# Weight loads on POOL's queue, weighted values right after the scores, and scatters that wait for them

## What is computed

```python
h = _layer_norm(x, ln1_w, ln1_b)
q, k, v = (einsum('btc,hcs->bhts', h, W) for W in (Wq, Wk, Wv))      # 4 heads of 32
wei = softmax(where(causal, einsum('bhts,bhus->bhtu', q, k) * scale, NEG_INF))
attn = einsum('bhtu,bhus->bhts', wei, v).transpose(0, 2, 1, 3).reshape(B, T, C)
x = x + attn @ Wo + bo
nx = _layer_norm(x, ln2_w, ln2_b)
noisy = nx @ Wr + br + noise * softplus(nx @ Wn + bn)
router_out = softmax(where(top 2 of 8 experts, noisy, NEG_INF))
for e in range(8):
    fe = relu(nx @ W1[e] + b1[e]) @ W2[e] + b2[e]                    # 128 -> 512 -> 128
    expert_out += router_out[..., e:e + 1] * fe
final = where(sigmoid(nx @ Wsk + bsk) <= 0.5, x + expert_out, x)
```

## Time and profile before

| | us |
|---|---|
| median of three runs | 997.89 |
| their lowest and highest | 996.54, 998.24 |
| the profiled execution | 997.75 |
| its span, first to last instruction | 995.2 |

### The profile page before, as it was taken

The page is one execution under the profiler, slowest core; times in us unless marked ns, Lnnn a source line. Parts: engine busy times, 40 slices in busy tenths (PEclk is TensorE's granted clock), DMA queues, the critical chain, the costliest instruction groups (busy, mean ns, idle before and its releaser), DMA issues.

```text
span 995.2 us, 19253 instructions
## 1 busy us (share of the span) xinstructions
PE 651.0 (65%) x4844; PEld 473.0 (48%) x4844; DVE 556.9 (56%) x2095; ACT 504.6 (51%) x1081; POOL 425.6 (43%) x490
## 2 busy tenths in 40 slices
PE   2477766775776766775775785419999999971000
PEld 1245553553553544553553553317777777760000
DVE  3364553553553553554554554337777777751998
ACT  3465554554554563554555543318778787760000
POOL 5223354354345354345345344633556565543000
PEclk9688777778678687678678776559999999996555
DMA  8744233233233242233233234466767667632998
GB/s 225 234 146 129 75 92 88 73 88 90 70 90 89 69 115 67 73 83 94 67 84 100 56 93 118 95 216 234 237 214 239 223 224 236 214 113 90 320 336 283
DMA packets 143292, 143.85 MB, mean 145 GB/s; under 512 B 25250, under 2 KB 113411, under 8 KB 143264
## 3 DMA queue, kind: packets, MB, share of 16 engines
q1 hardware_dynamic: 107744, 107.84, 36.6%
q10 hardware_dynamic: 23232, 19.93, 6.2%
q0 software_dynamic: 12288, 15.77, 5.1%
HBM read 73.86 MB, written 62.78 MB: 137 GB/s over the span
## 4 chain that ended last, share of the span: by engine, by line
PE 33%; issue 14%; DVE 6%; SPq 3%; another core or an unknown queue 2%; ACT 2%; DVEq 2%; DMA 1%; POOL 0%; POOLq 0%; ACTq 0%
PE ps L573 5%; PE ps L612 3%; PE ps L702 3%; PE ps L700 3%; DVE z L1160 2%; PE ps L701 2%; PE ps L712 2%; PE ps L713 2%; PE ps L714 2%; PE ps L621 2%; PE ps L655 2%; DVE z L1165 2%; PE ps L604 2%; PE ps L602 1%
## 5 line engine op out<-in xcount | busy, mean ns | idle before, releaser
L1238 POOL DMA_INDIRECT expert_rows<-pay,rows_of x256 | 252.4, 986 | 321.4 <-DVE rows_of L1050 248.8
L1255 POOL DMA_INDIRECT expert_results<-z,words x128 | 130.9, 1022 | 121.9 <-DVE z L1127 89.6
L743 ACT ACTIVATE z<-xres,shift,rstd 128x128 f32 (+1 forms) x256 | 105.0, 482 | 48.0 <-DVE shift L989 37.5
L612 PE MATMUL ps<-hlo,v_sb 128*32 128x128 f32 x1024 | 79.9, 383 | 72.1 <-issue 68.3
L995 DVE TENSOR_REDUCE smax<-ps 128x16 f32<-128x512 f32 x32 | 22.1, 691 | 182.1 <-remote 182.1
L1141 DVE TENSOR_TENSOR hlo<-h,hhi 128x512 fp32r<-128x512 f32 x128 | 88.6, 692 | 59.6 <-ACT hhi L887 48.5
L885 ACT ACTIVATE h<-ps,w1x 128x512 f32<-128x512 f32 x128 | 88.8, 694 | 47.9 <-PE ps L702 37.5
L612 PEld LDWEIGHTS ps<-hlo,v_sb 128*32 128x32 f32 x1024 | 49.8, 152 | 123.7 <-issue 116.4
L887 ACT ACTIVATE hhi<-ps,w1x 128x512 fp32r<-128x512 f32 x128 | 88.4, 691 | 0.0
L787 ACT ACTIVATE qT<-ps 128x512 f32<-128x512 f32 x32 | 19.0, 593 | 125.5 <-remote 110.9
L602 PE MATMUL ps<-hT,wq 128*128 128x512 f32 x64 | 46.1, 766 | 45.0 <-issue 38.4
(11 more groups left out here) (156 smaller groups left out, 1408.1 us busy)
## 6 DMA issues: line engine op xcount, KB each, us to landing
w1x<-split_weights SPq DMA_DIRECT2D x33, 514.0 KB
w2x<-split_weights SPq DMA_DIRECT2D x33, 512.5 KB
expert_results<-zeros SPq DMA_DIRECT2D x32, 512.0 KB
pay<-expert_rows SPq DMA_DIRECT2D x33, 264.0 KB
xres<-in_r_x SPq DMA_DIRECT2D x32, 256.0 KB, 5.1
hhi<-kT SPq DMA_DIRECT2D x128, 64.0 KB
hlo<-pT SPq DMA_DIRECT2D x128, 64.0 KB
hhi<-expert_results SPq DMA_DIRECT2D x16, 512.0 KB, 6.0
```

The source lines that it names most:

```text
L612: m = nc.tensor.matmul(ps[h * HS:(h + 1) * HS, O_BANK, j * P:(j + 1) * P], v_sb[:, odd, j, h * HS:(h + 1) * HS], p_bd[:, :, (j * H + h) * ...
L743: m = nc.scalar.activation(z[:, j:j + 1], tile(xres, n, j), ACT.Identity, bias=shift[:, which, j:j + 1], scale=rstd[:, which, j:j + 1])
L1238: g.indirect_dma_start(rows, bass.IndirectOffsetOnAxis(ap=rows_of[:, odd, k * J + j:k * J + j + 1], axis=0), pay[:, odd, k, j, :], None, b ...
L1255: g.indirect_dma_start(results, bass.IndirectOffsetOnAxis(ap=words[:, slot, j:j + 1], axis=0), yrow[slot][:, j, :], None, bounds_check=K * ...
```

## The change

- **PE's order.** The 32 matmuls of the weighted values stand right behind the scores, ahead of q and k.
- **POOL's hold.** Before a group's eight scatters (group n = t - 3, step t) POOL also waits for `s_o_made` of n + 4, which is the weighted values of group t, done in PE's step t + 1.
- **The rank** is summed by 6 matmuls in place of 15, with the running counts in one more column block, so that DVE copies `fill` (instead of adding).
- **The payload** of group n is copied in step n + 3 (before: n + 2).
- **Waits of DVE** for z1 and z2 move from ahead of the statistics to ahead of `rstd`.
- **First steps.** `load_raw` goes to POOL's queue: four experts ahead of the loop, the others as their slot is free. `store_cut` goes to SP's queue, behind `spread_k`. DVE zeroes `k_bd` (t = -2) and `p_bd` (t = -1). The scale of the first norm has a semaphore of its own, so it waits for two small loads and not for the q, k and v weights.

```diff
--- before.py
+++ after.py
@@ -205,6 +205,7 @@
...
         s_p_bd = sem("p_bd")
+        s_norm1_in = sem("norm1_in")
@@ -344,7 +345,7 @@
...
         SENT = 16 * K * J
-        QKV = 16 * 5
+        QKV = 16 * 3
@@ -458,6 +459,8 @@
...
                     spread_k(n)
+                for e in splits(t - 1):
+                    store_cut(e)
@@ -467,21 +470,19 @@
...
 
-            def load_raw(e):
-                slot = e % 4
-                sp.dma_start(raws[slot][:, 0:HF], W1[e]).then_inc(raw_in[slot], 16)
-                sp.dma_start(raws[slot][:, HF:2 * HF].rearrange("p (k c) -> p k c", c=C),
-                             W2[e].rearrange("(k p) c -> p k c", p=P)).then_inc(raw_in[slot], 16)
+            def store_cut(e):
+                sp.wait_ge(s_cut_low, e + 1)
+                for w, split in enumerate((wsplit1, wsplit2)):
+                    sp.dma_start(split[e * P:(e + 1) * P, 0:2 * HF], wcut[e % 4][:, w].bitcast(F32)
+                                 ).then_inc(cut_out[e % 4], 16)
...
             load_first(0, s_x_early[0])
-            sp.dma_start(norm1[:, 0:1], ln1_w.unsqueeze(1)).then_inc(s_qkv_in, 16)
-            sp.dma_start(norm1[:, 1:2], ln1_b.unsqueeze(1)).then_inc(s_qkv_in, 16)
+            sp.dma_start(norm1[:, 0:1], ln1_w.unsqueeze(1)).then_inc(s_norm1_in, 16)
+            sp.dma_start(norm1[:, 1:2], ln1_b.unsqueeze(1)).then_inc(s_norm1_in, 16)
...
             load_first(1, s_x_early[1])
-            load_raw(0)
-            load_raw(1)
@@ -594,15 +595,6 @@
...
                     m.then_inc(s_s_made, 1)
-                n = t + 1
-                if live(n):
-                    pe.wait_ge(s_hT_made, n + 1)
-                    if isinstance(n, int) and n == 0:
-                        pe.wait_ge(s_qkv_in, QKV)
-                    nc.tensor.matmul(ps[:, 4, :], wq[:].rearrange("c h s -> c (h s)"), hT[:],
-                                     start=True, stop=True).then_inc(s_q_made, 1)
-                    nc.tensor.matmul(ps[:, 6, :], wk[:].rearrange("c h s -> c (h s)"), hT[:],
-                                     start=True, stop=True).then_inc(s_k_made, 1)
@@ -616,6 +608,15 @@
...
                 if live(n):
+                    pe.wait_ge(s_hT_made, n + 1)
+                    if isinstance(n, int) and n == 0:
+                        pe.wait_ge(s_qkv_in, QKV)
+                    nc.tensor.matmul(ps[:, 4, :], wq[:].rearrange("c h s -> c (h s)"), hT[:],
+                                     start=True, stop=True).then_inc(s_q_made, 1)
+                    nc.tensor.matmul(ps[:, 6, :], wk[:].rearrange("c h s -> c (h s)"), hT[:],
+                                     start=True, stop=True).then_inc(s_k_made, 1)
+                n = t + 1
+                if live(n):
@@ -625,17 +626,14 @@
...
                     wait(pe, s_route, n * ROUTE)
-                    nc.tensor.matmul(ps[:, 7, 384:384 + J * E1].rearrange("p (j e) -> p j e", e=E1), ones_row[:],
-                                     fill[0:1].unsqueeze(1).to_broadcast([1, J, E1]), start=True, stop=False)
-                    for j in range(J):
-                        rank = ps[:, 7, 384 + j * E1:384 + (j + 1) * E1]
-                        nc.tensor.matmul(rank, before[:], hot_any[:, j, :], start=False, stop=False)
-                        for i in range(j):
-                            nc.tensor.matmul(rank, ones[:], hot_any[:, i, :], start=False,
-                                             stop=(i == j - 1 and j == J - 1))
-                    for j in range(J):
-                        m = nc.tensor.matmul(ps[:, 7, 384 + J * E1:384 + (J + 1) * E1], ones[:], hot_any[:, j, :],
-                                             start=(j == 0), stop=(j == J - 1))
+                    counts = ps[:, 7, 384:384 + (J + 1) * E1].rearrange("p (j e) -> p j e", e=E1)
+                    nc.tensor.matmul(counts, ones_row[:], fill[0:1].unsqueeze(1).to_broadcast([1, J + 1, E1]),
+                                     start=True, stop=False)
+                    nc.tensor.matmul(counts[:, 0:J], before[:], hot_any[:], start=False, stop=False)
+                    for i in range(J):
+                        m = nc.tensor.matmul(counts[:, i + 1:J + 1], ones[:],
+                                             hot_any[:, i].unsqueeze(1).to_broadcast([P, J - i, E1]),
+                                             start=False, stop=(i == J - 1))
@@ -819,12 +817,12 @@
...
                                          ACT.Copy).then_inc(s_v_copied, 1)
-                n = t - 2
-                if live(n):
-                    wait(act, sent[par], pair(n, par, SENT))
+                n = t - 3
+                if live(n):
+                    wait(act, sent[odd], pair(n, odd, SENT))
...
                         act.wait_ge(s_pay_zeroed, 1)
-                    nc.scalar.activation(pay[:, par, :, :, 0:C], z2[:, par].unsqueeze(1).to_broadcast([P, K, J, C]),
+                    nc.scalar.activation(pay[:, odd, :, :, 0:C], z2[:, odd].unsqueeze(1).to_broadcast([P, K, J, C]),
@@ -836,10 +834,6 @@
...
                     nc.scalar.activation(tiles(top2, n), top[:, :, 0:K], ACT.Copy).then_inc(s_top_kept, 1)
-                for e in splits(t - 1):
-                    store_cut(e)
-                    if e + 4 < E:
-                        load_raw(e + 4)
@@ -847,20 +841,6 @@
...
 
-            def load_raw(e):
-                slot = e % 4
-                act.dma_start(raws[slot][:, 0:HF], W1[e]).then_inc(raw_in[slot], 16)
-                act.dma_start(raws[slot][:, HF:2 * HF].rearrange("p (k c) -> p k c", c=C),
-                              W2[e].rearrange("(k p) c -> p k c", p=P)).then_inc(raw_in[slot], 16)
-
-            def store_cut(e):
-                act.wait_ge(s_cut_low, e + 1)
-                for w, split in enumerate((wsplit1, wsplit2)):
-                    act.dma_start(split[e * P:(e + 1) * P, 0:2 * HF], wcut[e % 4][:, w].bitcast(F32)
-                                  ).then_inc(cut_out[e % 4], 16)
-
-            load_raw(2)
-            load_raw(3)
@@ -946,11 +926,9 @@
...
                             apart(dve, (x_in[par], pair(t + 2, par, 16) + 16 - 8 * EARLY))
-                        wait(dve, s_z1, t + 2)
...
                             apart(dve, (s_x1_made, n + 1))
-                            wait(dve, s_z2, n)
@@ -960,8 +938,11 @@
...
                 if isinstance(t, int) and t == -2:
-                    turn_scale(norm1, s_qkv_in, QKV)
+                    ev.memset(k_bd, 0.0).then_inc(s_bd_zeroed, 1)
+                    turn_scale(norm1, s_norm1_in, 32)
                     make_masks()
+                if isinstance(t, int) and t == -1:
+                    ev.memset(p_bd, 0.0).then_inc(s_bd_zeroed, 1)
@@ -983,6 +964,10 @@
...
                     dve.wait_ge(s_norm, base + 3)
+                    if live(t + 2):
+                        wait(dve, s_z1, t + 2)
+                    if live(t - 2):
+                        wait(dve, s_z2, t - 2)
@@ -1032,8 +1017,7 @@
...
                     dve.wait_ge(s_rank_made, n + 1)
-                    ev.tensor_tensor(fill[:], fill[:], ps[:, 7, 384 + J * E1:384 + (J + 1) * E1],
-                                     ALU.add).then_inc(s_route, 1)
+                    ev.tensor_copy(fill[:], ps[:, 7, 384 + J * E1:384 + (J + 1) * E1]).then_inc(s_route, 1)
@@ -1177,6 +1161,13 @@
...
             g = nc.gpsimd
+
+            def load_raw(e):
+                slot = e % 4
+                g.dma_start(raws[slot][:, 0:HF], W1[e]).then_inc(raw_in[slot], 16)
+                g.dma_start(raws[slot][:, HF:2 * HF].rearrange("p (k c) -> p k c", c=C),
+                            W2[e].rearrange("(k p) c -> p k c", p=P)).then_inc(raw_in[slot], 16)
+
@@ -1215,8 +1206,8 @@
...
                    allow_small_or_imprecise_dtypes=True).then_inc(s_token_next, 1)
-            g.memset(k_bd, 0.0).then_inc(s_bd_zeroed, 1)
-            g.memset(p_bd, 0.0).then_inc(s_bd_zeroed, 1)
+            for e in range(4):
+                load_raw(e)
@@ -1232,7 +1223,8 @@
...
                     apart(pool, (s_route, n * ROUTE + ROUTE),
-                                (s_pay_made, n + 1))
+                                (s_pay_made, n + 1),
+                                (s_o_made, upto(n + 4)))
@@ -1242,6 +1234,9 @@
...
                 slot = e % 4
+                if 1 <= e <= 4:
+                    pool.wait_ge(s_cut_low, e)
+                    load_raw(e + 3)
```

## The result

The kernel before took 998.69 us (median of 6 runs) beside the changed kernel's **953.13 us** (944.21 to 956.34): a ratio of 0.954, 95% interval 0.949 to 0.958. The direction is the predicted one; the time lies 8 us above the range of 852 to 945. The profiled execution took 956.34 us, span 954.6.

The account below looks back on a forecast made before the run. The prediction took 32-column matmuls, stalled while POOL scatters, to bound the pipeline at 18.7 us a group. Its sum was 997.75 - 99.5 (period) - 4 (first steps) - 4 (drain) = 890 us, range 852 to 945.

Parts of the forecast that it names:

- Mechanism: In the pipeline, POOL's scatters hold back matmuls on 32 columns some ten microseconds; full-width ones pass with a small lag.
- Period: Time per group in the pipeline: 18.7 us falls to 15.0 (13.5 to 16.5), worth -99.5 us over 27 distances.
- The loop through the hold: Weighted values' end, 0.8 us to first scatter, 10.0 of scatters, 1.98 to release, then scores and weighted values: 15.0 us.
- 1.98 + 1.5 + 0.7: After a group's last scatter: narrow matmuls finish (1.98 us), weighted values run (1.5), ACT and DVE hand-offs lag (0.7).
- First steps: Start of the pipeline: moved loads, stores and zeroing free ACT and start scores earlier, -4 us, between -12 and +8.
- the sign of the +8: First four steps: spreads of pT landing behind the stores in SP's queue would show the +8 us bound.
- Drain: From the pipeline's last mask to its last scatter's end: 64.6 us becomes 60.3, -4 us, from -8 to +2.
- Counted as worth nothing: In the pipeline, the later payload copy, the shorter rank and DVE's moved waits were each put at nothing.
- central case: Only narrow matmuls stall, so the hold shortens the pipeline's groups to 15.0 us: 890 us, recorded bounds 850 to 935, chance 0.74.
- Rival 1: Inside the pipeline's scatter stretch every signal lags, not PE's alone: 17.5 us a group, 957 us; chance 0.14.
- Rival 2: Scatters stall all of PE's pipeline work, decided once over 5.9 us must wait: 22.3 us a group, 1095 us; chance 0.08.
- Rival 3: No contention in the pipeline, the hold only moves the stall: groups stay at 18.7 us, 990 to 998 us; chance 0.04.

Follow-up runs that it names:

- e12: The changed kernel without POOL's hold, with a test stretch of matmul and ScalarE trials ahead of its pipeline: 1260.9 us, one execution (kernel before 997.1).
- e4: The kernel before with the first steps' part of the change alone: 774.4 us against 782.5, ratio 0.990.
- e7: The kernel before with first steps and POOL's hold, old order, payload not moved, plus an added test stretch: 1157.6 us, one execution (kernel before 782.4).
- e11: The kernel before with first steps, POOL's hold and the later payload, in the old order of TensorE: 784.7 us against 782.0, ratio 1.004.
- e9: The changed kernel without POOL's hold, with a test stretch ahead of its pipeline: 926.3 us, one execution (kernel before 784.2).
- e5: The changed kernel itself, run again beside the kernel before in another sitting: 794.3 us against 781.8, ratio 1.016.

## Why the prediction was wrong, point by point

- **Mechanism.** It took the kind of matmul for the cause. The step that failed is "so full-width matmuls pass, with a small lag; those on 32 columns don't". The earlier trace rows showed stretches with few instructions beside the scatters (15 matmuls of the rank; 4.6 matmuls a microsecond in the experts' stage, 903 in 195 us), and I read their width instead of their number. The runs showed in its place that full-width matmuls are held back as well: z2's transposes by 4.5 us and the projection by 6.5 us in the changed kernel's step, and 8.7 us over e12's trial of short full-width matmuls.
- **Period, 15.0 predicted, 17.0 measured: 54 of the 66 us by which the profiled execution lies over 890.** The loop through the hold is right, with 0.9 us from weighted values to scatter and 10.0 us of scatters. The term mis-sized is the stretch from the last scatter's end to the next weighted values' end: 1.98 + 1.5 + 0.7 = 4.2 us by the sum, 6.0 measured on average (17.0 - 10.1 - 0.9). In the sum the scores were released at once; in the step above the late z2 transposes and projection first let the logits (402.16) and the next transposes go, and only then the mask (404.43). Work that was put beside the scatters did not fit beside them.
- **What the sum got right.** smax's wait vanished, POOL is released by the weighted values, q and k finish inside the scatters, the first mask comes at 27.0 us (before 31.3). DVE wasn't next.
- **First steps: -4 predicted, +1.2 measured**, inside the bounds of -12 to +8, by the very wait named as the sign of the +8. Under the old order the same edits bring 8.1 us (e4, a free sitting): the two halves of the change spoil each other.
- **Drain: -4 predicted, +4.2 measured.** The bound of +2 was too tight. Of the sum's 60.3 us, the 16.7 to the first of the last four groups' scatters became 20.2 (550.6 to 570.8), and the four groups took 48.7 in place of 43.6, with gaps between them. The hold alone costs 6.3 us of drain in a free sitting.
- **Counted as worth nothing:** the rank and the moved waits were never run alone, so this isn't shown for them. For the payload it was wrong: its move breaks a ring worth 9 us a group (e7 and e11, free sittings).
- **The range.** The central case's own bounds (periods of 13.5 to 16.5 us, first steps -12 to +8, drain -8 to +2) add up to 838 to 949 us, not to the recorded 850 to 935. The measured time lies above this too.
- **Rivals.** Rival 1, "inside the stretch every signal lags, not PE's alone", gave 957 us and had 0.14; it comes nearest in mechanism, since ACT is held back too (e12). That its time is so near is in part luck: its 17.5 us a group is too long by 13 us over 27 distances, and its -8 for first steps and drain too low by 13. Rival 2's point of decision never came, since some of PE's work does pass. Rival 3, no contention, was given 0.04; it is what seven of eleven sittings show, with its consequence, a change that gains nothing (+1.6%).
- Of the Trainium skill's rule ("SBUF — State Buffer", "Who interferes with whom"), that no DMA contends with a compute engine and that TensorE and ScalarE wait on nobody: the free sittings agree (in e9 the 32-column batches take 18.6 us beside scatters and 18.4 beside plain DMAs), the blocked ones don't (10.9 and 5.7 us for a burst of 8), though no run tells whether it is the memory's ports that are in the way.

**What stays open** is what makes a sitting blocked. It is constant within one, changes on the same chip, concerns both engines tried (PE, ACT), and needs POOL's scatters. The loading of instructions is an unlikely cause: the DMA view of the changed kernel from 91 to 550 us has 9 packets on the instruction queues, too few for 27 groups that all wait. Every time here comes with a record of its execution, so no run tells whether the recording itself takes part. The Trainium skill describes such a path ("NOTIFIC — the notification-queue block", section "7.1 Overflow: three behaviours, one of which stalls the engine"): the records that engines leave go through a block whose inner stages push back when they fill and can throttle an engine. That would fit a count of instructions of any kind; no run here shows it.

## What to carry to other kernels

A stall that follows one engine's instructions may be counted in the other engines' instructions and not in their kind or time: before a schedule is built on "this kind passes", compare the number of instructions that each observed stretch held. A wait added to an engine that releases buffers can close a ring through a third engine's queue; follow each semaphore of the held transfers to whoever waits for it, and move those waits with it. And run the kernel before beside every measurement, on more than one occasion: the same change was worth -4.6% in one kind of sitting and +1.6% in the other.

## What the runs showed of the hardware that was not expected

- The same kernel on the same chip took 999 us in one sitting and 782 in another. In the changed kernel (953 and 794 us) the scatters of the pipeline account for nearly all of such a difference (812.7 and 804.3 us without them).
- In a blocked sitting eight scatters (0.97 us each, 1.28 apart) hold back both engines tried (e12): after some 28 to 65 of TensorE's instructions its signals come late, and ScalarE advances by four instructions in 1.42 us. Eight plain DMAs issued by POOL in 4.33 us hold back nobody.
- TensorE's records don't show it: of the projection's matmuls the record ends 6.5 us before DVE read their result, with "remote" as the only trace of it.
- The granted clock in the pipeline follows the gaps: 0.76 before, 0.81 after, 0.95 in e5's free sitting (90 to 400 us).
